# A second layer's projection of three chunks moved between the blocks of the first layer's experts

## The reference, cut to what matters

```
for l in range(2):                      # 16 heads of 8 dimensions, causal over 2048 tokens
    x = x + attn(ln(x, ln1[l]), wq[l], wk[l], wv[l], wo[l], biases[l])
    h = ln(x, ln2[l])
    # l = 0: each token's best 2 of 8 experts, all 8 computed; l = 1: one pair for the whole sequence
    x = x + moe(h, gate[l], w1[l], w2[l])
```

## Time and profile before

| | |
|---|---|
| median of 3 runs | 3186.29 us (3185.91 to 3187.24) |
| the profiled execution | 3188.68 us, its span 3187.0 us |
| TensorE busy | 2671.6 us (84%) |
| VectorE busy | 2630.8 us (83%) |
| ScalarE busy | 2250.3 us (71%) |
| GpSimd busy | 584.2 us (18%) |
| experts of f0, first up to last turning back | 588.0 to 804.1 us |
| experts of g0 | 2455.0 to 2670.5 us |
| first scan of f1, of g1 | 842.34 us, 2710.18 us |

### The profile page before, as it was taken

The page is one execution under the profiler, slowest core; times in us unless marked ns, Lnnn a source line. Parts: engine busy times, 40 slices in busy tenths (PEclk is TensorE's granted clock), DMA queues, the critical chain, the costliest instruction groups (busy, mean ns, idle before and its releaser), DMA issues. The chain is left out here.

```text
span 3187.0 us, 71816 instructions
## 1 busy us (share of the span) xinstructions
PE 2671.6 (84%) x28144; PEld 1170.0 (37%) x28144; DVE 2630.8 (83%) x3510; ACT 2250.3 (71%) x4330; POOL 584.2 (18%) x1115
## 2 busy tenths in 40 slices
PE   4468999799689995759999999489998997899976
PEld 3322333577323333512222223232333775323325
DVE  5668899777699995769999999389998776899976
ACT  1137888677378884539999998358987665589874
POOL 3133100444221001100000000132102542321011
PEclk8669999999799997969999999789999998799997
DMA  1061000211500000230000000330000212300001
GB/s 32 1 152 39 21 14 12 64 42 40 136 26 23 16 12 25 65 70 9 13 13 12 12 13 12 81 85 23 19 12 29 64 41 77 91 24 16 18 12 30
DMA packets 109757, 119.04 MB, mean 37 GB/s; under 512 B 20662, under 2 KB 87532, under 8 KB 109420
## 3 DMA queue, kind: packets, MB, share of 16 engines
q1 hardware_dynamic: 100780, 96.63, 11.1%
q0 software_dynamic: 4480, 13.90, 2.0%
q10 hardware_dynamic: 4160, 3.93, 0.6%
HBM read 70.31 MB, written 43.78 MB: 36 GB/s over the span
## 5 line engine op out<-in xcount | busy, mean ns | idle before, releaser
L1252 ACT ACTIVATE h_probsf<-h_ps_scoresf 128x512 f32<-128x512 f32 (+3 forms) x1216 | 603.3, 552 | 171.8 <-PE h_ps_scoresf L1194 160.5
L1252 ACT ACTIVATE h_probsg<-h_ps_scoresg 128x512 f32<-128x512 f32 (+3 forms) x1216 | 603.3, 552 | 160.7 <-PE h_ps_scoresg L1194 149.3
L1252 ACT ACTIVATE h_probsb<-h_ps_scoresb 128x512 f32<-128x512 f32 x1024 | 556.3, 596 | 95.2 <-PE h_ps_scoresb L1194 85.4
L1216 PE MATMUL h_ps_valuesf<-h_probsf,v_all 128*9 128x256 f32 (+2 forms) x4608 | 352.4, 378 | 37.5 <-POOL h_probsf L1342 30.2
L1216 PE MATMUL h_ps_valuesg<-h_probsg,v_all 128*9 128x256 f32 (+2 forms) x4608 | 350.8, 377 | 27.9 <-POOL h_probsg L1342 20.3
L1216 PE MATMUL h_ps_valuesb<-h_probsb,v_all 128*9 128x256 f32 x4096 | 318.1, 382 | 9.3 <-ACT h_drainedb L1261 4.6
L1297 DVE TENSOR_REDUCE h_maxima_0b<-h_ps_scanb 128x2 f32<-128x1024 f32 x256 | 292.5, 1216 | 27.3 <-PE h_ps_scanb L1156 27.3
L1297 DVE TENSOR_REDUCE h_maxima_2b<-h_ps_scanb 128x2 f32<-128x1024 f32 x256 | 292.8, 1217 | 6.4 <-PE h_ps_scanb L1156 6.3
L1297 DVE TENSOR_REDUCE h_maxima_0f<-h_ps_scanf 128x2 f32<-128x1024 f32 x224 | 259.2, 1218 | 21.4 <-PE h_ps_scanf L1156 20.8
L1297 DVE TENSOR_REDUCE h_maxima_0g<-h_ps_scang 128x2 f32<-128x1024 f32 x224 | 259.0, 1217 | 19.3 <-PE h_ps_scang L1156 18.7
L1156 PE MATMUL h_ps_scang<-k_stack,q_stack 48*128 48x512 bf16 (+3 forms) x1280 | 220.0, 364 | 36.0 <-DVE h_ps_valuesg L1267 9.1
(11 more groups left out here) (423 smaller groups left out, 4349.6 us busy)
## 6 DMA issues: line engine op xcount, KB each, us to landing
q_stack<-combine_weights SPq DMA_DIRECT2D x64, 256.0 KB, 3.2
q_stack<-in_L_ffn_e_w SPq DMA_DIRECT2D x24, 256.0 KB, 3.7
q_stack<-q_parts SPq DMA_DIRECT2D x20, 256.0 KB, 5.6
k_stack<-k_parts SPq DMA_DIRECT2D x20, 256.0 KB, 7.7
attended<-h_drainedf SPq DMA_DIRECT2D x16, 256.0 KB, 2.2
attended<-h_drainedf SPq DMA_DIRECT2D x32, 128.0 KB, 1.9
attended<-h_drainedb SPq DMA_DIRECT2D x32, 128.0 KB, 1.9
attended<-h_drainedg SPq DMA_DIRECT2D x16, 256.0 KB, 2.2
```

What stands on the lines that cost most here:

```text
L1216: last = nc.tensor.matmul(ps_values[32 * j:32 * j + VD, low:high], m.v_all[:, kb, QUAD * quad + j, :], probs[:, (u + j % banks) % RING_P, ...
L1252: nc.scalar.activation(by_head(probs[:, of % RING_P, :], of), by_head(ps_scores[:, of % RING_S, :], of), ACT.Exp, scale=SOFTMAX_SCALE).the ...
```

## The change

Both layers of a network now stand in one block, and the projection of layer 1 is done by a new class, `EarlyProjection`. For chunks 0, 1 and 2 its pieces are put at steps of layer 0's expert loop (the table `NEXT`); for chunk 3 they follow the experts in `end`. Its scratch (`hn`, `h_t`, `rest`, and one chunk's `parts` instead of two) lies in chunks 2 and 3 of `k_stack`, whose ones GpSimd sets again in `end`, before the loads of chunk 2. It has two banks of PSUM, those of `e_ps_turn`, in turns with the experts' own use; queries, keys and values of chunk 0 share one of them. `cw_rows`, `y_sb` and `acc` move to the upper half of `q_stack`, so that chunks 0 and 1 can be loaded into the lower half while the experts still run. The semaphores of the experts are cleared later, at GpSimd's 41st mask. In `attention_heads` SP's loads of chunks 2 and 3 come two moves later.

```
+NEXT_DEVIATION = 1
+NEXT = ({"normalise": 58, "turn": 62, "keep": 63, "q": 66, "high_q": 67, "rest_q": 68, "mid_q": 69, "low_q": 70,
+         "k": 72, "high_k": 73, "rest_k": 74, "mid_k": 75, "low_k": 77, "v": 78, "keep_v": 80},
+        {"normalise": 79, "turn": 84, "keep": 85, "q": 92, "high_q": 93, "rest_q": 94, "mid_q": 95, "low_q": 96,
+         "k": 93, "high_k": 94, "rest_k": 95, "mid_k": 96, "low_k": 97, "v": 99, "keep_v": 101},
+        {"normalise": 110, "turn": 114, "keep": 115, "q": 118, "high_q": 119, "rest_q": 120, "mid_q": 121, "low_q": 122,
+         "k": 119, "high_k": 120, "rest_k": 121, "mid_k": 122, "low_k": 123, "v": 124, "keep_v": 125})
+NEXT_WRITES = {19: [(0, 0, part) for part in range(3)], 21: [(0, 1, part) for part in range(3)],
+               26: [(1, k, part) for part in range(3) for k in range(2)],
+               31: [(2, k, part) for part in range(3) for k in range(2)]}
+NEXT_LOADS = (25, 28)
+NEXT_LOAD_BY_POOL = 25
...
-        raw_w2, y_sb, acc = second.raw, borrow(2, CH), borrow(2, CH)
+        raw_w2 = second.raw
         if by_token:
             t = router_tiles(borrow, P, TPC)
-            cw_rows, cw_t = borrow(RING_CW, CH), borrow(CH)[0:E]
+            cw_t = borrow(CH)[0:E]
+            borrowed.skip_to(CHUNKS * PAIRS * CH // 4)
+            cw_rows = borrow(RING_CW, CH)
...
@@ VectorE, after the statistics of chunk c, and in the loop
+                        if c < end:
+                            following.moments(step, c)
...
+                if due(k, "normalise") is not None:
+                    following.normalise(dve, due(k, "normalise"))
+                for i, name in enumerate("qk"):
+                    if due(k, "rest_" + name) is not None:
+                        following.residue(dve, due(k, "rest_" + name), i)
+                for i, name in enumerate("qk"):
+                    if due(k, "low_" + name) is not None:
+                        following.low(dve, due(k, "low_" + name), i)
+                if due(k, "keep_v") is not None:
+                    following.keep_v(dve, due(k, "keep_v"))
...
@@ GpSimd, in its loop over the experts' results y
+                    if following and c and e == NEXT_DEVIATION:
+                        following.deviation(pool, c - 1)
+                    if following and y == NEXT_LOAD_BY_POOL:
+                        following.load(pool, 1, 1)
...
@@ TensorE, before the turning back of chunk 2 and of chunk 3
+                    if following and k // blocks == end:
+                        pe.wait_ge(following.rest_ready, 4)
+            if following:
+                pe.wait_ge(following.v_kept, end)
...
@@ EarlyProjection.end, chunk 3: GpSimd, VectorE and TensorE
+                self.deviation(pool, c)
+                pool.wait_ge(*experts_done["weighted"])
+                buffers.pad(nc, m)
+                pool.wait_ge(m.named["h_padded"], len(buffers.layouts))
+                pool.wait_ge(self.v_ready, CHUNKS)
+                for k in range(2):
+                    pool.wait_ge(self.written[k][c % 2], 16 * 3 * (c // 2 + 1))
+                for i, low in enumerate((32, 32 + HALF)):
+                    nc.gpsimd.memset(m.k_stack[low:low + 32, 2:CHUNKS, :, :].bitcast(F32), BF16_ONES)\
+                        .then_inc(self.ones_back, 1)
+                    pool.wait_ge(self.ones_back, i + 1)
...
+                self.moments(Steps(dve, self.steps), c)
+                self.normalise(dve, c)
+                for k in range(2):
+                    self.residue(dve, c, k)
+                for k in range(2):
+                    self.low(dve, c, k)
+                self.keep_v(dve, c)
...
+                pe.wait_ge(self.rest_ready, 2 * c)
+                self.turn(pe, c)
+                pe.wait_ge(*experts_done["added"])
+                for k in range(2):
+                    self.product(pe, c, k)
+                self.product_v(pe, c)
...
@@ EarlyProjection, the values and the loads
+    def product_v(self, pe, c):
+        pe.wait_ge(self.rest_ready, 2 * c + (2 if self.banks[c][3] is self.banks[c][2] else 1))
...
+    def load(self, queue, c, b):
+        m, cols = self.m, slice(c * CH, (c + 1) * CH)
+        if c == 2:
+            queue.wait_ge(self.ones_back, 2)
...
@@ attention_heads: SP and GpSimd
-                if causal and k < CHUNKS - EARLY:
-                    projected["load"](sp, EARLY + k, 0)
+                if causal and 0 <= k - late < CHUNKS - EARLY:
+                    projected["load"](sp, EARLY + k - late, 0)
...
+                if k == STALE_AT:
+                    for s in stale:
+                        pool.sem_clear(s)
...
@@ feed_forward
-    for number in range(LAYERS):
-        last = number == LAYERS - 1
-        layer(nc, m, f"{n}{number}", number, first=number == 0, last=last,
-              load_experts=load_experts and number == 0, out=out if last else None)
+    with nc.Block() as m.block:
+        following = EarlyProjection(nc, m, 1)
+        done = layer(nc, m, f"{n}0", 0, first=True, load_experts=load_experts, following=following)
+        layer(nc, m, f"{n}1", 1, last=True, out=out, early=(following, done))
```

More of the change, by code:

```diff
@@ L1371, in sums @@
                 finish.load(sp, c)
+            late = 2 if stale else 0
             if not causal:
@@ L1641, with experts @@
 TURN_BACK = 7
-def experts(nc, m, n, layer, last, finish, attended, rows, second, h, borrowed, out=None):
+NEXT_DEVIATION = 1
[10 more added lines that the diff above has]
+NEXT_LOAD_BY_POOL = 25
+def experts(nc, m, n, layer, last, finish, attended, rows, second, h, borrowed, out=None, following=None):
     by_token = layer == 0
@@ L1705, in ps_logits, with due @@
             return ps_turn[:, c % 2, 0:TPC * E].rearrange("p (t e) -> p t e", e=E)
+        if following:
+            one, two = ps_turn[:, 0, :], ps_turn[:, 1, :]
+            following.banks = {0: (one, one, one, one), 1: (one, two, one, two), 2: (one, two, one, two)}
+        def due(k, what):
+            for c, at in enumerate(NEXT if following else ()):
+                if at[what] == k:
+                    return c
+            return None
         def prepared(k, offset):
@@ L1960, in turn_cw, with next_turn, next_q, next_k @@
                 last_.then_inc(cw_turned, 1)
+            def next_turn(c):
+                if c == 0:
+                    pe.wait_ge(cw_kept, end)
+                elif c == 1:
+                    pe.wait_ge(following.v_kept, 1)
+                else:
+                    pe.wait_ge(added, end)
+                following.turn(pe, c)
+            def next_q(c):
+                if c == 1:
+                    pe.wait_ge(cw_kept, CHUNKS)
+                elif c == 2:
+                    pe.wait_ge(following.v_kept, 2)
+                following.product(pe, c, 0)
+            def next_k(c):
+                if c == 0:
+                    pe.wait_ge(following.rest_ready, 1)
+                following.product(pe, c, 1)
             def turn_back(c):
@@ L2068, in _ @@
                             second.load(sp, E - LATE_SPLITS + y - FIRST_ROWS)
+                        if following:
+                            for of, k, part in NEXT_WRITES.get(y, ()):
+                                following.write(sp, of, k, part)
+                            if y == NEXT_LOADS[0]:
+                                for b in range(2):
+                                    following.load(sp, 0, b)
+                            if y == NEXT_LOADS[1]:
+                                following.load(sp, 1, 0)
             else:
@@ L2090, in _, with layer @@
                     sp.wait_ge(written, 16 * CHUNKS)
-def layer(nc, m, n, number=None, first=False, last=False, load_experts=False, out=None):
+    return {"weighted": (weighted, n_exp * CHUNKS), "added": (added, CHUNKS)}
+def layer(nc, m, n, number=None, first=False, last=False, load_experts=False, out=None, early=None, following=None):
     mixing = number is None
     across = HEADS * CH // P
-    with nc.Block() as m.block, ExitStack() as whole:
+    stale = m.stale("experts", "rows", "w2") if early else ()
+    with ExitStack() as whole:
         h = [whole.enter_context(nc.sbuf_tensor(x + n, [P, CHUNKS, CH], F32R)) for x in ("e_h_hi", "e_h_lo")] \
@@ L2121, in layer, with mixing_layer @@
         if not mixing:
[L2122 removed]
+            return experts(nc, m, n, number, last, finish, attended, rows, second, h, borrowed, out, following)
 def feed_forward(nc, m, n, load_experts=False, out=None):
[L2126 to L2129 removed]
+    with nc.Block() as m.block:
+        following = EarlyProjection(nc, m, 1)
+        done = layer(nc, m, f"{n}0", 0, first=True, load_experts=load_experts, following=following)
+        layer(nc, m, f"{n}1", 1, last=True, out=out, early=(following, done))
+def mixing_layer(nc, m, n):
+    with nc.Block() as m.block:
+        layer(nc, m, n)
 def build(nc, ins, out):
```

170 lines of the change are left out of this document (163 added, 7 removed).

## The result

The change made the kernel slower: 3193.5 us as the median of 7 runs (3190.39 to 3201.15) against 3186.29 before in as many (3184.48 to 3190.47), a ratio of 1.0023 [1.0013, 1.0032]. The forecast was 3165.0 us, with 3153.0 to 3180.0 as its range. The profiled execution took 3197.04 us, its span 3195.3.

A forecast was written before the change was run, and what follows sets the result against it. Between layers engines work by turns; the experts are TensorE's. Per network 22.2 (gap) + 1.0 (attention start) - 9.2 (TensorE's work) - 3.5 (stalls) = 10.5; twice, 21.0 off 3186.3 gives 3165 us, range 3153 to 3180.

The forecast's parts named there:

- The gap, 22.2 us a network: From f0's last transposes to f1's first scan, 38.92 us would fall to 16.7; same taken for g.
- TensorE's added work, 9.2 us a network: In the expert loop, transposes, products and values add 3.05 us a chunk over three chunks, in full on the path.
- The stalls, 3.5 us a network: In the expert loop, TensorE's extra waiting for VectorE's and ScalarE's added work, ranging from 0.5 to 9 us.
- 2.0 us more of waiting there, 0.5 each for the parts of chunks 0, 1 and 2: Expert loop: 2.0 us at step 88, the choice of experts, plus 0.5 per chunk; together 3.5 us a network.
- VectorE's 23.0 of idle: Expert loop: VectorE's idle plus 9.2 us of new TensorE work exceeds its added 19.2 us, though not all rightly placed.
- the bound of 9: Expert loop: the most that the stalls were taken to cost, in us per network.
- The prediction's second case: Expert loop: GpSimd's SBUF work stretches VectorE's moments and low parts, 5 us a network seen by TensorE; 3175 us, chance 0.13.
- "Clearing the semaphores at the 41st mask costs nothing": GpSimd in the attention: clearing costs nothing beside 8 us of gaps in its masks.
- The start of the attention, 1.0 us gained: After f1's first scan: row of maxima leaves sooner, GpSimd takes back 1.2 us; 1.0 gained, from -2 to 2.3.
- about 12.5: Start of the attention: GpSimd's first mask would come 12.5 us after the first scan instead of 16.0.
- four blocks 5.5 us: SP's queue in the expert loop: a result takes four blocks, 5.5 us; rows of weights are issued four results ahead.
- "Slower" had 0.06, for a VectorE that paces the loop: Fourth case, expert loop: VectorE paces wherever new work stands, all its 19.2 us are waited for; 3199 us, chance 0.06.

The follow-up runs named there:

- All four runs: Kernel before plus unused tile: 192 B ahead of the stacks 1.0026, 512 B there 0.9993, 192 B behind all tiles 0.9995; changed kernel, scratch tile 512 B: 0.998.
- the last version: Changed kernel with clearing beside the ones, moments on GpSimd, combine weights turned at step 26, chunk 1's projection at steps 90 to 104: 3158.14 us, 0.9906.
- the kernel with both repairs: Changed kernel with semaphore clearing moved beside the settings of ones and moments of chunks 0 to 2 on GpSimd: 3167.88 us, 0.9939.

## Why the prediction was wrong

*The gap, 22.2 us a network: right.* It gave 21.3 and 23.2, together the 44.4 forecast.

*TensorE's added work, 9.2 us a network: right.* TensorE's busy time says 16.3, of which 7.2 are clock, and 10.4 where the clock is as before; doubling the products cost 15 us where their durations make 15.7.

*The stalls, 3.5 us a network: wrong.* The step that failed is "2.0 us more of waiting there, 0.5 each for the parts of chunks 0, 1 and 2". It looked for the trouble at the choice of experts near step 88, where 1.10 us came. The waits came at steps 41, 73 and 105, where the moments follow sum and statistics in one piece: 6.1 us in f and 5.0 in g. I had counted the moments as 1.5 us of VectorE's 23.0 of idle, a sum over the loop; here they made a piece of 3 to 4 us in which VectorE served nobody. The loops of before and of the three kernels with an unused tile took 213.6 to 215.5 us, and five of the six loops of the change 231.3 to 232.6: some 17 longer, less 9.2 leaves about 8 us a network where 3.5 stood, near the bound of 9. The sixth, f in the profile of after, is 22.7 longer, which leaves 13.5, because about 7 us more went to a low clock. Why it fell there and not in the other five, with the same waits, is open. With the moments on GpSimd the term is 1 to 2 us a network.

The Trainium skill, page "SBUF — State Buffer", section "Who interferes with whom", which the prediction weighed for operations with two SBUF inputs, says that a VectorE `tensor_scalar` in its two-port mode locks the shared ports just as well. The trace agrees for both: in f the moment that was caught took 1.28 us instead of 0.16 in chunks 0 and 2 (L303, two inputs) and 1.21 instead of 0.17 in chunk 1 (L302, one input), and the normalising of chunk 1, with one input too, took 3.17 us for four operations at 737.80 instead of 1.1. The prediction's second case had this mechanism, at 5 us a network, for two moments and a low part in each chunk. One moment was caught, and by the 18 places above it made about 1 us of each wait, up to 3 us a network. The case was right in kind, and stood at 0.13.

*"Clearing the semaphores at the 41st mask costs nothing": wrong.* The clears stand one behind the other in GpSimd's stream, 4.68 us, and the gaps between its masks are 0.2 to 1.3 us each. That these add up to 8 us does not help, as TensorE comes for each mask in turn. Before, the clearing stood behind the power of 2.91 us, and only 0.50 us of idle time followed there (810.47 to 810.97). In its new place it cost 6.3 and 4.7 us by the profiles, 11 in all; by the ratios it is 0.15% or 5 us with the moments on VectorE (1.0023 to 1.0008) and 0.24% or 8 us with them on GpSimd (0.9963 to 0.9939).

*The start of the attention, 1.0 us gained: about right, for partly wrong reasons.* From first scan to first scores it is now 13.84 us in f where it was 14.73, and 14.33 in g where it was 14.92. The row of maxima still takes 5.4 us (853.27 to 858.7). GpSimd's loads are issued at 852.98, just ahead of it, and I take them to be the reason, which no run tried; they start earlier than I had them, since the last write, issued at 843.15, had landed by 845.18, within about 2 us and not 6.2. The prediction's "about 12.5" for the first mask does not follow from its own terms either: 16.0 less the 2.35 that TensorE gains is 13.7, when GpSimd is free too. Nor are four blocks 5.5 us; by the earlier trace rows they are 48 / 32 x 4 = 6.0. Neither slip moves the sum by more than 1.2 us a network.

*The layout: not considered at all.* The tile of 192 B costs 0.26% by itself, about 8 us, and removing it from the changed kernel gave 1.0023 to 0.998, from the last version 0.9906 to 0.9887: 6 to 14 us. In the compiled programs `q_stack` begins at byte 80384 of a partition in the kernel before, a multiple of 256, as does `k_stack` with 113152. The 192 B put both 192 bytes past one; 512 B, or a tile behind them, do not. Those are the tiles that parts are loaded into, in rows of 1 KB. The Trainium skill, page "DMA: Bandwidth & Descriptors", section "How a descriptor splits into AXI transactions", says that a descriptor which does not start at a multiple of 256 B fetches from the boundary below it and pays for the bytes ahead. All four runs agree with 256 B as the step that counts. They do not show that fetching is the mechanism: that rule is told of what is read, while the stacks are what the loads write. The transfers of 128 KB are 0.5 to 1.5 us slower in the rows above, and the writes from the parts to DRAM most of all, though `p_partsb` starts at 96 bytes past a multiple before and at 32 past one both in the kernel with 192 B ahead (7.6 and 7.6 us) and in the one with 192 B behind (6.7 and 6.6). So the parts' own address is not the cause, and how the loads' targets would slow the writes is open. No run shifted the stacks alone either, so that it is these two tiles, and not the weights between, was not tried.

*The sum, mended.* For the two networks, with loops as in the five profiles that agree: gaps 44.4, TensorE's work -18.4, waits and clock about -16, clearing -5 to -11, layout about -8, the start of the attentions 1.5. That is -1.5 to -7.5, and the ratio says -7.3. With the loop of f as the profile of after has it, the waits and clock are some -22 and the sum is 6 lower. The parts were measured one by one and overlap in what they spoil, so the sum closes only within some 6 us. Some stages also differ by 2 to 7 us between profiles without a line in them changed (the first chunk of f0's experts is 2.4 us shorter in the kernel with both repairs), which I could not explain.

*The chances.* "Slower" had 0.06, for a VectorE that paces the loop. It does not: the doubled products show that. The kernel became slower by three costs, of which only the stalls were among the cases with a price above zero.

## What to carry to other kernels

Room on an engine is a matter of place, not of sum: before work is put beside a stream that feeds TensorE, look for the longest piece in which that engine would serve nobody, and compare it with the depth of the ring. Here, with a ring of four, a piece of 3 us made TensorE wait 1 us and one of 4 us made it wait 2. Take a stage's time from several profiles before a part of it is explained: one loop of six was 6 us longer than the rest. And put nothing of odd size ahead of tiles that DMAs fill; a change that adds a tile is to be compared with the kernel before plus that tile.

## What the runs showed of the hardware

- Waits of 1 to 2 us in a stream in which TensorE is busy about 90% of the time did not lower the clock by themselves: in five of six loops with them the granted clock was 0.95 to 0.96, as before, and in one it was 0.93, which cost 7 us.
- A VectorE operation of 4 columns took 1.2 to 1.3 us instead of 0.17 when it met GpSimd's of 512 columns (1.27 to 1.31), with one SBUF input as well as with two.
- Clearing the network's stale semaphores holds GpSimd's stream for 4.68 us, and nothing when issued behind a running operation.
- 192 B of unused SBUF cost 0.26% [0.16, 0.35]; with 512 B at the same place the time was 0.07% lower, which is no change [-0.16, 0.02]. The plain attention alone took 657.8 to 658.8 us in the eight kernels whose stacks start off a multiple of 256 B, and 654.7 to 655.7 in the six whose stacks start at one.
- Eight operations of 4 columns take GpSimd 1.7 us, hardly more than the 1.5 that VectorE was counted with.
